# Turning returned results in another PSUM bank, and another order of the first loads

## What is computed

```python
x = x + conv_ref(_ln_c(x), ...)      # sign -> 2x3 conv -> bn -> relu, twice, + input, relu
t = _to_tokens(x)                    # 16 x 1024 tokens of 64 numbers
t = t + ffn_ref(_ln_t(t), ...)
# ffn_ref: probs = softmax(x @ gate_w + gate_b); the two best experts of each token, weights renormalised
#   hidden = silu(x @ w1[e]) * (x @ w2[e]);  out = sum over the two e of weight * (hidden @ w3[e])
x = _from_tokens(t, x)
```

## Time and profile before

| | |
|---|---|
| time, median of 3 runs | 526.46 us (525.55 to 528.04) |
| the profiled execution | 528.78 us, span of its trace 527.0 us |
| busy share of the span | PE 90%, PE weight load 80%, DVE 84%, ACT 76%, GpSimd 56% |
| mean granted clock of TensorE | 0.927 of full |
| chain that ended last | PE 70%, DVE 15%, issue 5%, DMA 4%, ACT 3% |
| queue of SP and ACT (q1) | 23.84 MB in 52208 packets, with ACT's (q10) 7.29 MB in 1584 |

### The profile page before, as it was taken

How to read it: one execution, slowest core, us unless ns; L and a number is a source line. 1 busy time by engine, 2 the same in 40 slices (tenths; PEclk the granted TensorE clock), 3 DMA queues, 4 the chain that set the end, 5 groups by cost and what they waited for, 6 DMA issues and landing times.

```text
span 527.0 us, 14225 instructions
## 1 busy us (share of the span) xinstructions
PE 471.7 (90%) x4186; PEld 420.4 (80%) x4186; DVE 441.1 (84%) x1242; ACT 399.7 (76%) x946; POOL 293.1 (56%) x378
## 2 busy tenths in 40 slices
PE   6799999999996444899999999999999999999982
PEld 5467767775774433799999999999999999999972
DVE  5567787987978988899999999998988989989882
ACT  4686787986965321699999999997998979889760
POOL 4000006777777777777766666655544545555552
PEclk9879799998998756899999999999999999999996
DMA  7981011121100004430132322242422534210324
GB/s 266 328 157 40 1 42 45 47 70 51 46 30 29 29 29 92 87 75 31 46 81 54 68 50 57 62 103 62 119 62 45 132 64 147 67 32 17 95 90 159
DMA packets 62664, 40.97 MB, mean 78 GB/s; under 512 B 50003, under 2 KB 54318, under 8 KB 62080
## 3 DMA queue, kind: packets, MB, share of 16 engines
q1 hardware_dynamic: 52208, 23.84, 19.8%
q0 software_dynamic: 8800, 8.94, 5.1%
q10 hardware_dynamic: 1584, 7.29, 3.5%
HBM read 21.46 MB, written 19.19 MB: 77 GB/s over the span
## 4 chain that ended last, share of the span: by engine, by line
PE 70%; DVE 15%; issue 5%; DMA 4%; ACT 3%; SPq 1%; POOL 1%; POOLq 0%; DVEq 0%; ACTq 0%
PE up L968 15%; PE up L970 12%; PE turn L984 11%; PE up L802 8%; PE lines L1001 6%; PE small L818 4%; PE small L847 3%; PE small L949 3%; PE lines L1003 3%; DMA x_in<-in_x 3%; PE up L777 2%; PE up L788 1%; PE turn L841 1%; DVE match L1272 1%; POOL results L519 1%
## 5 line engine op out<-in xcount | busy, mean ns | idle before, releaser
L519 POOL DMA_INDIRECT results<-result,page_in x147 | 156.4, 1064 | 110.4 <-ACT xc L703 84.1
L498 POOL DMA_INDIRECT pages<-payload,slot_int x128 | 130.7, 1021 | 106.6 <-DVE slot_int L1411 68.3
L968 PE MATMUL up<-up_w,xs_hi 128*128 x588 | 160.1, 305 | 3.9 <-DVE hidden L1591 2.4
L970 PE MATMUL up<-up_w,xs_lo 128*128 x588 | 147.5, 284 | 0.0
L968 PEld LDWEIGHTS up<-up_w,xs_hi 128*128 128x128 f32 x588 | 112.2, 191 | 7.3 <-issue 4.8
L703 ACT ACTIVATE xc<-up 128x512 f32<-128x512 f32 x147 | 90.9, 619 | 34.7 <-PE up L970 33.4
L970 PEld LDWEIGHTS up<-up_w,xs_lo 128*128 128x128 f32 x588 | 112.9, 192 | 0.0
L1586 DVE SCALAR_TENSOR_TENSOR hidden<-up,page_in,xc 128x128 f32<-128x128 f32 x196 | 59.5, 345 | 16.4 <-ACT xc L703 15.7
L1596 DVE TENSOR_TENSOR hidden_lo<-turn,hidden_hi 128x512 f16<-128x512 f32 x98 | 67.5, 689 | 0.2
L716 ACT ACTIVATE hidden_hi<-turn 128x512 f16<-128x512 f32 x98 | 62.7, 640 | 0.0
L984 PE MATMUL turn<-ident,hidden 128*128 128x128 f32 x392 | 59.3, 274 | 0.8 <-DVE up_raw L1619 0.7
(11 more groups left out here) (262 smaller groups left out, 979.4 us busy)
## 6 DMA issues: line engine op xcount, KB each, us to landing
pages<-up_w ACTq DMA_DIRECT2D x4, 1332.0 KB, 11.0
page_in<-pages SPq DMA_DIRECT2D x147, 36.0 KB
page_in<-pages SPq DMA_DIRECT2D x147, 32.0 KB
x_in<-in_x SPq DMA_DIRECT2D x7, 512.0 KB, 3.4
out<-up_raw SPq DMA_DIRECT2D x5, 512.0 KB, 3.7
results<-result,page_in POOLq DMA_INDIRECT x147
up_raw<-in_L_ffn_w SPq DMA_DIRECT2D x4, 512.0 KB, 17.4
pages<-payload,slot_int POOLq DMA_INDIRECT x128, 2.2
```

What stands on the lines that cost most here:

```text
L498: pool.indirect_dma_start(out=pages, out_offset=bass.IndirectOffsetOnAxis(ap=slot_int[q % PAYLOADS][:, t:t + 1], axis=0), in_=payload[q % ...
L519: pool.indirect_dma_start(out=results, out_offset=bass.IndirectOffsetOnAxis(ap=page_in[g % LOADS][:, k, D + AT_TOKEN:D + AT_TOKEN + 1].bit ...
L968: pe.matmul(target, xs_hi[g % 2][:, k * P:(k + 1) * P], weights[:, bass.ds(e * 2, 2 * HID)], start=True, stop=False)
L970: last = pe.matmul(target, xs_lo[g % 2][:, k * P:(k + 1) * P], weights[:, bass.ds(e * 2, 2 * HID)], start=False, stop=True)
```

## The change

Four things change. (1) back_step moves to n = 75 + 16q + 4c, always the last page of a group, and the transposes go into the bank `small`, behind the down product of that iteration. They wait for xs_ready (rows_low has read `small`), and turn_rows of the group after waits for back_read. The two old waits, on lo_done and in turn_hidden, are gone. (2) load(1) is issued right after the convolution weights. (3) `blank` lies on the memory of the last three pairs of x2; GpSimd makes it after its other tables, SP sends it behind down_raw and ahead of load(2). ACT no longer issues it, nor does make_hi(0) wait for it; the residual of pair 5 does. (4) Counts of tables_made fall by two.

```diff
-    back_step = {TILES * q + 74 + 2 * c: (q, c) for q in range(EARLY) for c in range(CH)}
+    back_step = {TILES * q + 75 + BY * c: (q, c) for q in range(EARLY) for c in range(CH)}
@@ sync
             sp.dma_start(conv_raw[C:P, :], w2.rearrange("o c i j -> o (c i j)")).then_inc(conv_in, 16)
+            load(1)
             for i, v in enumerate((gamma1, beta1, mean1, var1, gamma2, beta2, mean2, var2)):
...
             sp.dma_start(gate_bias[:, :], gate_b.partition_broadcast(P)).then_inc(gate_in, 16)
-            load(1)
...
             sp.dma_start(down_raw[:, :, :], ffn_w3.rearrange("e h d -> h e d")).then_inc(down_in, 16)
+            sp.wait_ge(blank_made, 2)
+            for part in range(4):
+                sp.dma_start(pages.rearrange("(p part r) w -> part p r w", p=P, part=4)[part], blank)\
+                    .then_inc(blanked, 16)
             for q in range(2, PAIRS):
                 load(q)
@@ gpsimd
+            pool.memset(blank, 0.0).then_inc(blank_made, 1)
+            pool.wait_ge(blank_made, 1)
+            pool.memset(blank[:, :, AT_TOKEN:AT_TOKEN + 1].bitcast(I32), NOWHERE).then_inc(blank_made, 1)
             pool.wait_ge(blanked, 64)
@@ scalar
-            act.wait_ge(tables_made, 2)
-            for part in range(4):
-                act.dma_start(pages.rearrange("(p part r) w -> part p r w", p=P, part=4)[part], blank)\
-                    .then_inc(blanked, 16)
...
                 if m == 0:
-                    act.wait_ge(blanked, 64)
                     act.wait_ge(up_in[0], 32)
@@ tensor, turn_rows(g)
+                if BY * (g - 1) - 1 in back_step:
+                    q, c = back_step[BY * (g - 1) - 1]
+                    pe.wait_ge(back_read, CH * q + c + 1)
@@ tensor, turn_hidden(n)
-                if n + 1 in back_step:
-                    q, c = back_step[n + 1]
-                    pe.wait_ge(back_read, CH * q + c + 1)
@@ tensor, down_product(n)
                     pe.wait_ge(result_ready, max(GROUPS - 2, last_ready(n - 2)))
+                    if n == LAST + 1:
+                        pe.wait_ge(back_read, CH * EARLY)
@@ tensor, the loop over n
-                if n in back_step:
-
-                    q, c = back_step[n]
-                    pe.wait_ge(lo_done, n - 2)
-                    turn_back(c, q, turn[(n - 1) % 2])
                 if 0 <= n - LAG < PAGES:
                     down_product(n - LAG, experts.pop(n - LAG))
+                if n in back_step:
+                    q, c = back_step[n]
+                    pe.wait_ge(xs_ready, n // BY + 2)
+                    turn_back(c, q, small)
@@ vector
-            dve.memset(blank, 0.0).then_inc(tables_made, 1)
-            dve.wait_ge(tables_made, 1)
-            dve.memset(blank[:, :, AT_TOKEN:AT_TOKEN + 1].bitcast(I32), NOWHERE).then_inc(tables_made, 1)
...
+                if q == BLANKED:
+                    dve.wait_ge(blanked, 64)
...
-                    add_input(c, q, turn[(n - 1) % 2][:, :])
+                    add_input(c, q, small[:, :])
```

More of the change, by code:

```diff
@@ L74, in metaformer_kernel @@
     KNOWN = PAIRS - 3
+    BLANKED = PAIRS - 3
     SURE = 64
@@ L134, in metaformer_kernel @@
         down_w = sb("down_w", [P, E, STRIDE], F16)
-        blank = up_w[:, :, :, :].rearrange("p e m h -> p (e m h)").bitcast(F32)[:, 0:37 * ROW]
-        blank = blank.rearrange("p (r w) -> p r w", w=ROW)
         largest = sb("largest", [P, 3], F32)
@@ L159, in metaformer_kernel @@
         x2 = sb("x2", [P, PAIRS, HW], F32)
+        blank = x2[:, BLANKED:PAIRS, :].rearrange("p q n -> p (q n)")[:, 0:37 * ROW]
+        blank = blank.rearrange("p (r w) -> p r w", w=ROW)
         logits = sb("logits", [P, TILES, E], F32)
@@ L262, in metaformer_kernel @@
         first_loaded = [sem(f"first_loaded{c}") for c in range(CH)]
-        blanked = sem("blanked")
+        blank_made, blanked = sem("blank_made"), sem("blanked")
         pool_made, dve_made, tables_made = sem("pool_made"), sem("dve_made"), sem("tables_made")
@@ L916, in _ @@
                     if r == 0:
-                        pe.wait_ge(tables_made, 12)
+                        pe.wait_ge(tables_made, 10)
                     count(r)
@@ L1031, in _ @@
                     experts[n + 1] = experts_of(n + 1)
+                if 0 <= n - LAG < PAGES:
+                    down_product(n - LAG, experts.pop(n - LAG))
                 if n in back_step:
                     q, c = back_step[n]
-                    pe.wait_ge(lo_done, n - 2)
-                    turn_back(c, q, turn[(n - 1) % 2])
-                if 0 <= n - LAG < PAGES:
-                    down_product(n - LAG, experts.pop(n - LAG))
+                    pe.wait_ge(xs_ready, n // BY + 2)
+                    turn_back(c, q, small)
             for q in range(EARLY, PAIRS):
@@ L1124, in make_tables @@
                     .then_inc(tables_made, 1)
-                dve.wait_ge(tables_made, 6)
+                dve.wait_ge(tables_made, 4)
                 dve.tensor_copy(place[:, 4:6], place_bits[:, 4:6]).then_inc(tables_made, 1)
-                dve.wait_ge(tables_made, 7)
+                dve.wait_ge(tables_made, 5)
                 dve.tensor_scalar(place[:, 0:1], place[:, 4:5], 1.0, 2.0, ALU.is_equal, ALU.mult)
@@ L1131, in make_tables @@
                 dve.tensor_scalar(place[:, 2:3], place[:, 4:5], 3.0, None, ALU.is_equal).then_inc(tables_made, 1)
+                dve.wait_ge(tables_made, 6)
+                dve.tensor_reduce(place[:, 3:4], place[:, 0:3], AX.X, ALU.add).then_inc(tables_made, 1)
+                dve.wait_ge(tables_made, 7)
+                dve.tensor_copy(place_bits[:, 6:7], place[:, 3:4]).then_inc(tables_made, 1)
                 dve.wait_ge(tables_made, 8)
-                dve.tensor_reduce(place[:, 3:4], place[:, 0:3], AX.X, ALU.add).then_inc(tables_made, 1)
-                dve.wait_ge(tables_made, 9)
-                dve.tensor_copy(place_bits[:, 6:7], place[:, 3:4]).then_inc(tables_made, 1)
-                dve.wait_ge(tables_made, 10)
             def more_tables():
```

## The result

The changed kernel took 518.67 us (median of 4 executions, 516.02 to 520.16), the kernel before on the same chip 527.25 us (4, 525.55 to 531.26): ratio 0.985 [0.980, 0.989]. The forecast was 519.2 us in a range of 516.2 to 523.0. The profiled execution took 519.35 us, with a span of 517.5 us and a mean granted clock of 0.930.

What follows compares the result with a forecast made beforehand. Bounds: a load first, then a PE, ACT and DVE chain, PE alone from about 210 us, GpSimd writes at the end. Gains of 5.1 (page loop) and 2.2 (start), 7.3 us off 526.5, gave 519.2, range 516.2 to 523.0.

Steps and rivals of the forecast that it cites:

- Part 1, a step at 0.48 us: Page loop, turning results back: each step costs 0.48 us in place of 1.0; gain 5.1 us in all.
- DVE keeps 0.4 us: Page loop: DVE has 7.8 us of work in a step's group of 8.25, so it stays under PE.
- The last step: Moved to page 143: DVE's 0.66 us delay the last 11 writes, PE's 0.44 are hidden; cost 0.7 us.
- SP's stores and loads at the end: SP's queue: pair 4's store comes some 6 us later, with a store and two loads behind it; cost 0.
- Part 2, center of the second pair at 16.8: Start: with its load early and parts 2 and 3 together, PE's center at 16.8 in place of 21.29.
- Part 3, ACT's sign at 7.0: Start: without issuing blank rows, ACT's sign of the first pair starts at 7.0, 2.0 us earlier; 1.5 come through.
- What is late next, third pair at 37.3: Start: the third pair's load, behind the blank rows on SP's queue, holds its center until 37.3, not 35.0.
- Gain of 2.2 us from the start: Parts 2 and 3 together: third pair's center at 37.3 in place of 39.5, 2.2 us, between 1.4 and 3.7.
- Clock: Rival: twelve convolutions behind the third pair's new wait run at 1.2 GHz, 2.6 us lost, 521.8; chance 0.2.
- No wait for the third pair: Rival, start: blank rows faster or cut short, so the full 4.5 us come, 516.9; chance 0.12.
- Steps don't gain: Rival, page loop: another wait at the same price replaces the old one, only 2.2 us gained, 524.3; chance 0.05.
- DVE as the bound: Rival, page loop: add_input makes rows_low a page late, a step costs 2.5 us, 539; chance 0.03.

Runs made afterwards that it cites:

- the loop's part alone: Kernel before with only the page loop's new back_step place, waits and bank, everything at the start as before: 520.99 us, ratio 0.992.
- two adds: Changed kernel with DVE's add of each of the ten steps in the page loop made twice: 520.84 us.
- Norm rows first: Kernel with the third pair's load ahead of the blank rows, plus the eight batch norm row loads ahead of the second pair's load: 515.63 us, ratio 0.983.
- the start's change alone: Changed kernel with the old back_step, turn bank and waits, so only loads and blank rows are in the new order: 527.41 us, ratio 1.004.
- second pair early: Kernel before with the new page loop and the second pair's load issued early, blank rows still on DVE and ACT: 518.00 us, ratio 0.991.
- the second comparison: The changed kernel itself run again on another chip: 518.14 us, kernel before 523.42 us, ratio 0.984.
- the blank rows' version: Changed kernel with the second pair's load back in its old place behind the gate's, so at the start only the blank rows are moved: 522.28 us, ratio 0.997.
- three adds: Changed kernel with DVE's add of each of the ten steps in the page loop made three times: 531.54 us.
- Third pair first: Changed kernel with the third pair's load issued ahead of the blank rows: 517.35 us, ratio 0.988.
- the last add later: Kernel with third pair and norm rows first, plus DVE's add of step 143 put behind add_halves of the next iteration: 516.87 us, ratio 0.975.

## Why the prediction was right, and where it was not

**What bounds, page loop.** Right. PE alone bounds it before and after; its busy time in the stretch is the whole stretch, 143.02 of 143.02.

**Part 1, a step at 0.48 us.** The mechanism is right: the waits of the earlier trace rows are gone, rows_low ends ahead of the transposes, plain groups keep their 7.77. The term is mis-sized. The prediction named the wait of 0.1 us at the seam and said that the up product behind the transposes no longer has it, but then added 0.44 + 0.04 and subtracted nothing. It had to be 0.41 less about 0.1, 0.31, below its own lower bound of 0.44 (and its upper bound of 0.66, "cold", was the length of a row and not a cost); the transposes done twice show it, 0.31 for the first four, 0.43 for the next. The nine steps in the loop were to cost 4.3; the stretch holds all ten, and they cost 143.02 - 18 x 7.77 = 3.2. From silu to silu the groups around a pair's two steps take 7.92, 8.09, 7.92 and 7.78, under the 8.2 to 8.4 of the forecast; with the end, 0.59 for 0.7, the gain is 6.35 us in the trace and 5.8 +- 0.4 in the times of the loop's part alone, for 5.1.

**DVE keeps 0.4 us.** Right, shown by two adds (0.41 to 0.46 of the second hidden) and three (nothing of the third hidden).

**The last step.** Right for DVE, 0.59 for 0.66, and it can be moved away (0.61 in the trace). PE's part was to be hidden behind the writes; it lies in the loop with the others (the last group takes 7.96 us from silu to silu, a plain one 7.77).

**SP's stores and loads at the end.** Nothing shows that the later stores cost anything: the writes are 1.29 us apart from the first to the last, as before.

**Part 2, center of the second pair at 16.8.** It came at 19.00 in one profile and 15.92 in another of the same kernel. The number had no error bar for PE's clock, and took bn_raw to be ready at 9.47 as in one profile before, which lay at 10.04 in the next with the same start: the variance product started at 10.42 and 9.69. What held it was PE's first center product, not the small loads, though these were now behind 0.5 MB, which the prediction didn't look at. Norm rows first gave 1.0 +- 0.7 us at equal clock, which shows nothing by itself.

**Part 3, ACT's sign at 7.0.** It was 7.32, and 7.15 in the other profile. Right, though the second half of it waited for center until 8.52.

**What is late next, third pair at 37.3.** Right to 0.1 us, 37.23 and 37.56, as is the reason: the wait on the DMA of x_in. The bytes ahead of it and their rate (0.4 MB a us, 417 GB/s measured) were read well.

**Gain of 2.2 us from the start.** Wrong, and this is the step that failed: "Now it is issued at 28.50 and lands 8.2 us later, at 36.7, and PE takes it at 39.5: 2.8 us of slack". The 39.5 came from one execution. The start of the kernel before, run with the new loop, had its third pair at 37.32, 0.4 us after the load, and the start's change alone is worth 0.5 +- 0.4 us at equal clock and nothing in plain times. The slack of 2.8 was not a property of the kernel but of that execution. The load landed at 36.7 and 36.9 before and at 37.2 to 38.1 with the new start, so moving PE's work forward, the second pair's center by up to 5.4 us (21.29 to 15.92), led to the same transfer. That this transfer is in the way is shown by putting it first: no wait in four profiles, a center 2.7 us earlier on the mean, and 2.0 +- 0.6 us.

**The queues.** The Trainium skill (DMA: Bandwidth & Descriptors, Queues, rings and completion order) has descriptors of one queue served in the order of issue. The runs agree: behind the blank rows on SP's queue the third pair lands at 37.2 to 38.6, ahead of them at 28.0, and with the blank rows on ACT's queue (second pair early) it lands at 35.0. For this load the two-queue order, which the change gave up, was better than the change's, and one queue with the load first is better still.

**The two errors cancel.** Part 1 gave 0.7 to 1.25 more than said, the start 1.7 less. The sum of 7.3 stands beside 6.6 +- 0.6 and 7.2 +- 0.5 at equal clock, and the two parts alone, -5.8 and -0.5, add up to -6.3. That the sum of the terms was right is luck, and so is a part of the 518.67 against 519.2: the forecast was taken off 526.46, while the 55 later executions of the kernel before have a median of 523.6, from which the same 7.3 give 516.3. In the plain means of the second comparison the change is 4.9 +- 1.9 us faster.

**The rivals.** Clock: not separable as stated. Low stretches come and go at the start from one execution to the next, in the kernel before too, and the mean time at 1.2 GHz is 69.0 us before and 70.3 and 73.4 after: at 0.40 us for each that is 0.5 and 1.8 us, in the direction of the rival and short of its 2.6; at this spread it isn't shown for the changed kernel alone. In the kept profiles the loss that it named can be seen. In the seven in which the third pair waits for its load (0.43 to 5.33 us, the blank rows' version among them), the eight center products behind the wait take 1.99 to 3.78 us, 3.3 on the mean; in the seven in which it doesn't wait, 1.89 to 2.73, mean 2.3. And in two of the former (blank rows alone, three adds) the next twelve convolutions take 4.11 and 4.07 us for 2.81. So a loss of about 1 us at this place, for which the sum had no term, is likely; the rival's full 2.6 us came in neither profile of the changed kernel. No wait for the third pair: false in both profiles. Steps don't gain: false. DVE as the bound: false for this change, right in kind, with too high a price.

**What stays open.** Why the new versions spend more time at 1.2 GHz than the kernel before, and so which part of the equal-clock gains a user would see. And whether the blank rows' part alone costs 0.8 us at all: its third pair lands 1.7 us later than in the kernel with the old start (38.6 for 36.9), and the clock is low behind it.

**The best version.** Third pair first and norm rows first: 515.63 us, 10.0 +- 0.5 us faster than the kernel before at equal clock (8.3 +- 1.1 by the plain means), 3 us faster than the change; what the norm rows add to it is 1.0 +- 0.7; with the last add later 516.87 us, ratio 0.975 to its own runs of before (the medians, 516.87 and 524.09, give 0.986), and no difference between the two that the times can tell.

## What to carry to other kernels

A slack read from one execution is slack at the clock that this execution had: before it is taken as cover or as a bound, look at what engine speed it assumes, and compare the absolute time at which the transfer lands with the earliest time at which the engine could ask for it. The same holds for a gain: 4.8 us in one pair of profiles were 2.7 on the mean of ten. When an instruction is placed where the engine already waits, subtract that wait from its price, and take as its price the time to the start of the next instruction and not the length of its row. When a load is moved ahead in a queue, list every small load that is now behind it, and look whether an engine really stands idle for one before blaming it. The best order tried here was norm rows, second pair, weights, third pair, and the bulk that nobody waits for last.

## What the runs showed of the hardware

One kernel's time spreads by 11 us (520.07 to 530.88 in 55 executions), and most of it goes with the time that TensorE spends at 1.2 GHz: 0.40 us for each us there, with 1.2 us of scatter left. In the profile of the kernel before, about 10 us at 1.2 GHz lie in the first 40 us, 22 from 40 to 175, 34 from 175 to 225 (PE busy 26.64 of 50 us there), none from 225 to 500 (busy 272.47 of 275), and 12 in the last 27 us (busy 15.35). Those that differ from one execution to the next are in part at the start: from 12 to 18 us the same kernel had a granted clock of 0.50 in one execution and 1.00 in another, with PE busy 6.00 and 5.37 us of six and 22 and 29 of its products recorded there, so a busy PE did its work more slowly.

The experts' weights, in pieces of 512 B and less, move at 214 GB/s with a DMA share of 1.21, the blank rows at 417 with a share of 1.00. For the order of a queue that makes a MB of weights twice as dear as a MB of blank rows.
